# Expert layer of a four-layer kernel: router pieces, the low part and the spreads take other places in VectorE's and TensorE's step

## The reference, cut to what matters

```python
raw_scores = einsum('bsd,ed->bse', u, centroids)           # 16 experts
s = softmax(raw_scores + expert_biases)
topk_vals, topk_idx = top_k(s, 2)
g_topk = sum(one_hot(topk_idx, 16) * topk_vals[..., None], axis=-2)
xe = einsum('bsd,eod->bseo', u, Wr) + br
routed = einsum('bse,bseo->bso', g_topk, xe)
shared = (einsum('bsd,eod->bso', u, Ws) + sum(bs)) / 2
return u + routed + shared
```

## Time and profile before

| | |
|---|---|
| time, median of 3 runs | 1394.78 us (1393.96 to 1395.35) |
| the profiled execution: time, its span | 1394.4 us, 1392.2 us |
| TensorE matmuls busy | 1273.8 us (91% of the span) |
| VectorE, ScalarE, GpSimd busy | 996.3, 768.2, 519.3 us |
| expert layer, from its first spread to its last pair | 322.6 to 523.2 us of the span |

### The profile page before, as it was taken

The page is one execution under the profiler, slowest core; times in us unless marked ns, Lnnn a source line. Parts: engine busy times, 40 slices in busy tenths (PEclk is TensorE's granted clock), DMA queues, the critical chain, the costliest instruction groups (busy, mean ns, idle before and its releaser), DMA issues.

```text
span 1392.2 us, 31560 instructions
## 1 busy us (share of the span) xinstructions
PE 1273.8 (91%) x10330; PEld 1050.0 (75%) x10330; DVE 996.3 (72%) x2481; ACT 768.2 (55%) x2324; POOL 519.3 (37%) x687
## 2 busy tenths in 40 slices
PE   3999999987898896999999999999999977899997
PEld 2777777767888885777777777777777755899997
DVE  5466666656888886767777777777777764788886
ACT  2233333322222222988888888888888886444442
POOL 3243333334454455434445454444444431111111
PEclk9999999997999998999999999999999999999999
DMA  8000000000000000000000000000000000000000
GB/s 266 1 1 1 0 0 0 0 1 1 1 0 0 0 1 1 2 1 2 1 2 2 0 0 0 0 0 0 0 0 0 1 1 1 1 12 11 11 11 17
DMA packets 14445, 12.30 MB, mean 9 GB/s; under 512 B 1922, under 2 KB 12708, under 8 KB 14116
## 3 DMA queue, kind: packets, MB, share of 16 engines
q1 hardware_dynamic: 14372, 11.35, 2.6%
HBM read 9.25 MB, written 2.10 MB: 8 GB/s over the span
## 4 chain that ended last, share of the span: by engine, by line
PE 55%; DVE 18%; issue 11%; ACT 9%; POOL 4%; DVEq 1%; POOLq 0%; ACTq 0%
PE bank L935 9%; PE bank L171 8%; PE bank L528 8%; PE bank L477 6%; PE bank L1015 6%; ACT work L952 6%; PE bank L1028 5%; PE bank L800 4%; DVE work L944 3%; PE bank L986 3%; DVE stat L278 2%; ACT work L972 2%; POOL rstd L345 2%; PE bank L755 2%; DVE work L1180 1%
## 5 line engine op out<-in xcount | busy, mean ns | idle before, releaser
L952 ACT ACTIVATE work<-bank,work 128x256 f32<-128x256 f32 x512 | 234.8, 485 | 70.4 <-DVE work L944 70.4
L944 DVE TENSOR_REDUCE work<-bank 128x2 f32<-128x512 f32 x256 | 158.8, 682 | 131.6 <-PE bank L935 131.6
L918 POOL TENSOR_TENSOR work<-work 128x512 f32<-128x512 f32 x128 | 160.6, 1276 | 88.9 <-DVE work L908 88.9
L343 POOL TENSOR_SCALAR ve<-mv 128x2 f32<-128x2 f32 x128 | 28.6, 223 | 362.5 <-DVE mv L283 362.5
L972 ACT ACTIVATE work<-work 128x256 f32<-128x256 f32 x384 | 161.5, 535 | 0.0
L966 POOL TENSOR_TENSOR work<-work 128x512 f32<-128x512 f32 x64 | 66.6, 1040 | 251.1 <-DVE work L960 251.1
L935 PE MATMUL bank<-work 32*128 32x256 f32 x2048 | 130.5, 391 | 14.3 <-ACT XnT L372 9.6
L486 DVE TENSOR_TENSOR la_work<-bank,tri 128x512 f32<-128x512 f32 x128 | 87.6, 684 | 77.3 <-PE bank L477 77.2
L986 PE MATMUL bank<-ident,work 128*128 128x128 f32 x1024 | 137.7, 277 | 2.3 <-ACT work L994 1.3
L1015 PE MATMUL bank<-work 128*64 128x256 f32 x1024 | 126.5, 388 | 14.0 <-DVE work L1001 14.0
L800 PE MATMUL bank<-WrT,moe_work 128*128 128x128 f32 x1024 | 137.6, 278 | 0.7 <-POOL moe_work L777 0.7
(11 more groups left out here) (170 smaller groups left out, 2924.2 us busy)
## 6 DMA issues: line engine op xcount, KB each, us to landing
X<-in_x SPq DMA_DIRECT2D x4, 512.0 KB, 6.1
wF<-in_L_ffn_h_w SPq DMA_DIRECT2D x2, 1024.0 KB, 9.8
out<-X SPq DMA_DIRECT2D x16, 128.0 KB, 1.8
w_qkv<-in_L_attn_w_qkv SPq DMA_DIRECT2D x1, 1536.0 KB, 8.9
WrT<-in_L_ffn_Wr SPq DMA_DIRECT2D x1, 1024.0 KB, 4.9
w_out<-in_L_attn_w_out SPq DMA_DIRECT2D x1, 512.0 KB, 10.2
wF<-in_L_ffn_w_w SPq DMA_DIRECT2D x2, 256.0 KB, 8.6
rope_sin<-in_rope_sin SPq DMA_DIRECT2D x1, 256.0 KB, 2.8
```

The costliest lines, as they stand in the source:

```text
L918: nc.gpsimd.tensor_tensor((QT if kind == "q" else KT)[:, p, a, :], rc[:, ru % 2, :], rs_[:, ru % 2, :], ALU.add).then_inc(c_rope, 1)
L944: nc.vector.tensor_reduce(nmax[:, QUAD * a + j, :], SB_[j][:, :].rearrange("p (t k) -> p t k", t=T), AX.X, ALU.max, negate=True).then_inc( ...
L952: ins = nc.scalar.activation(pr[:, a % 2, j, t, :], SB_[j][:, t * LEN:(t + 1) * LEN], ACT.Exp, bias=nmax[:, h, t:t + 1], accum_out=psum_[: ...
```

## The change

On VectorE the late router parts move from behind pair 4 to before it, right behind norm 1. Pair 5 moves behind norm 2, low from behind norm 4 to right behind pair 5. Early 0 comes before norm 5, early 1 right behind it, next 0 after that; early 2 comes before next 1 in place of after it, and early 3 and next 2 change places. On TensorE the transposes of the gates come after pair 1 and its spread in place of pair 2, and the next sequence's first four spreads go behind pairs 5, 6, 6 and 7 in place of 4, 5, 6 and 7. The work is the same, instruction for instruction.

```diff
-        MOE_ORDER = (("norm", 0), ("norm", 1), ("pair", 4), ("late", 4), ("late", 5), ("late", 6), ("late", 7), ("pair", 5),
-                     ("norm", 2), ("pair", 6), ("norm", 3), ("norm", 4), ("low", 0), ("norm", 5), ("next", 0),
-                     ("early", 0), ("norm", 6), ("norm", 7), ("early", 1), ("next", 1), ("early", 2), ("norm", 8),
-                     ("early", 3), ("next", 2))
+        MOE_ORDER = (("norm", 0), ("norm", 1), ("late", 4), ("late", 5), ("late", 6), ("late", 7), ("pair", 4), ("norm", 2),
+                     ("pair", 5), ("low", 0), ("pair", 6), ("norm", 3), ("norm", 4), ("early", 0), ("norm", 5), ("early", 1),
+                     ("next", 0), ("norm", 6), ("norm", 7), ("early", 2), ("next", 1), ("norm", 8), ("next", 2),
+                     ("early", 3))
...
                     elif more:
-                        moe_spread_tensor(pe, i + 1, 1 - p, k - 4)
+                        for k2 in ((), (0,), (1, 2), (3,))[k - 4]:
+                            moe_spread_tensor(pe, i + 1, 1 - p, k2)
                     if k == 0 and not i_is(i, 0, 1):
                         norm_tensor(pe, 2, i - 2)
-                    if k == 2 and more:
+                    if k == 1 and more:
                         moe_gates_tensor(pe, i + 1, 1 - p)
```

## The result

The changed kernel takes 1402.55 us (median of 6 runs, 1400.71 to 1404.75) against 1395.07 for the kernel before in the same comparison: a ratio of 1.0053, 95% interval 1.0040 to 1.0066. It is slower, as forecast, by 7.5 us, and 2.3 us above the forecast time of 1400.3 (the forecast's sum had +5.8). The profiled execution of the changed kernel took 1400.71 us, its span is 1398.8 us against 1392.2.

The account below looks back on a forecast made before the run. The prediction took a ring of VectorE and GpSimd as the bound. Twelve loop steps at +0.43 (+5.2 us) and +0.6 outside the loop made +5.8 on 1394.4, stated as 1400.3 us, with an 80% range of 1393.2 to 1402.8.

Parts of the forecast that it names:

- a ring with TensorE in slack: Expert layer loop: VectorE and GpSimd set the 12.59 us step; filling TensorE's 1.27 us hole gives nothing unless the ring shortens.
- Closing the holes: VectorE's step: the 0.48 hole before norm 3 goes, the one before norm 5 exceeds 1 us, about 0.3 appears before norm 8.
- TensorE's margin for VectorE's pair 6: Gates' transposes hold pair 2, spread 6 and VectorE's pair 6 at 3.87; ready by 3.8 at worst, the tightest margin, 0.1 us.
- The step's +0.43: End of VectorE's step: early 3's CAST is held until GpSimd's L777 ends, lengthening each loop step by 0.43 us; chance 0.56.
- the rival in which only L703 is held: At early 3 the product L703 is held but the CAST is not: +0.25 a step, +3.4 in all, 1397.9; chance 0.10.
- The sum: Whole kernel: twelve loop steps +5.2 us and four steps outside the loop +0.6, together +5.8; forecast time 1400.3 us.
- The four steps outside the loop: Steps 0, 1, 14 and 15 have only part of the loss: between -0.05 and +0.45 each, together +0.6 us.
- The next layer has nothing to absorb it: Behind the expert layer: the next layer starts from the last norm 8, so nothing of the +5.8 us is absorbed.
- That nothing is held: No hold at early 3, as L777 comes after it or the two don't exclude each other: 1393.7, no change; chance 0.17.
- That the late parts are held as well, or the gates' margin is gone: Late parts beside GpSimd, or gates' transposes on TensorE: 12 x 0.2 us more, 1403; chance 0.04.
- L323 might come first at norm 5: L323 ahead of L777: norm 5 about 0.6 instead of 1.40, 12 x -0.4, 1389.6; chance 0.08.
- TensorE as the bound: TensorE bounds the kernel after all and its 15.2 us wait goes: 1379; chance 0.05.

Follow-up runs that it names:

- the half product: Changed kernel with GpSimd's product L777 of pair 3 covering one expert of two in sequences 1 to 15 (128x256 instead of 128x512): 1395.16 us, ratio 1.0003.
- early 3 moved: Changed kernel with early 3 (L700, L703) right behind early 2 instead of at the end of VectorE's step: 1392.19 us, ratio 0.9979 to the kernel before.
- TensorE's part: Kernel before with only the change's TensorE order (gates behind pair 1, first spreads behind pairs 5, 6, 6, 7): 1398.32 us, ratio 1.0027.
- VectorE's part: Kernel before with only the change's VectorE order, TensorE's order as before: 1401.24 us, ratio 1.0044.
- both holds out: Changed kernel with early 3 behind early 2 and GpSimd's product of pair 7 waiting for norm 5: 1377.54 us, ratio 0.9871 to the kernel before.

## Why the prediction was right, point by point

**The bound.** VectorE and GpSimd were read as a ring with TensorE in slack. Right: TensorE's 15.2 us wait was removed and the step grew; and the ring's own arithmetic gave the new places of norm 2 to norm 8 to within 0.3 us. Norm 3 and norm 5 are the 0.3 late in step 6: norm 2 is 0.08 late, and low was taken at 0.35 because starts overlap ends, but no such overlap stands around it (pair 5 at 405.48, low at 406.19, pair 6 at 406.64: 1.16 us where 0.96 was summed).

**Closing the holes.** The 0.48 before norm 3 went, the one before norm 5 grew to 0.98 and 0.92 (above 1 forecast), a new one of 0.17 stood before norm 8 (0.3 forecast). Right, with the sizes somewhat off. TensorE's margin for VectorE's pair 6, which I put at 0.1 us, held: no wait stands there.

**Early 3.** The step's +0.43 was measured as +0.44 (26.06 less 25.18, halved), but its parts differ. The CAST is held, from 0.17 to 0.65 and 0.74 in the two steps of an iteration; of the bounds it was the upper one, and the rival in which only L703 is held is out. L777 comes 1.90 and 2.00 us behind early 2 where I had 1.89 from the earlier trace rows. The next piece follows the CAST's end by 0.18 inside an iteration and by 0.52 at its turn, where 0.28 was taken for both. The extra time of an iteration (0.22, of which 0.18 before pair 4) was said to stay in its first step; it did in size but now lies at the turn, as 0.26 before L278: the two steps are 12.95 and 13.11, not 13.1 and 12.9.

The prediction reads from its rows that small VectorE instructions are held until GpSimd's instruction ends. None of the meetings in them is one of a CAST, so for early 3 this was the author's estimate. Beside L777 the runs show it, the run with the half product most directly (the product is 0.64 us long, and the CAST ends 0.03 behind it). Beside GpSimd's power L345 they do not: products of two SBUF tiles ran beside it in 0.16 and 0.23 us, as without it (rows in the last section). What sets the two GpSimd instructions apart is not shown.

**The sum.** The sum itself is not closed: 1394.4 plus 5.8 plus the 0.4 by which the median was said to lie above the profiled execution is 1400.6, not 1400.3. Twelve loop steps: +5.2 forecast, +4.65 measured, since the first of them did not grow (12.97 before, 12.96 after) and the last, behind which the loop does not turn, grew by 0.30 (12.49 to 12.79). The four steps outside the loop: +0.6 forecast, +0.3 measured. "The next layer has nothing to absorb it" is the step that was mis-sized: the layer behind did not absorb, it added. From the last norm 8 to the first scores it is 1.1 us more and to the end 1.7. In the profiled executions the 4.9 of the expert layer and these 2.8, less 1.1 in the layer before, make +6.6; the medians differ by 7.5, and single executions can't settle the 0.9 between the two. So the expert layer paid 0.9 less than the 5.8 forecast for it, and the stretches behind it, put at nothing, paid 2.8. That the total came out only 1.7 above the forecast sum is in part luck, and at 1402.55 the time lies just inside the upper end of the range, 1402.8.

That opening takes 22.4 to 22.5 us in the changed kernel and in the runs with early 3 moved, the half product, TensorE's part and VectorE's part, and 21.2 to 21.4 in the kernel before and the other four. Nothing in it was changed. The granted clock of TensorE differs there between the kernel before and the changed one. Both in 5 us stretches, the kernel before first (the third column from the end is the granted clock, as a share):

```profile
525.00:530.00 5.00, 4.67 (x21) 4.05 (x21) 2.26 (x8) 1.16 (x2) 2.65 (x4) 0.70 0.00 0
...
550.00:555.00 5.00, 3.73 (x20) 2.40 (x20) 3.78 (x9) 4.69 (x19) 1.10 (x2) 0.91 0.01 2
```

```profile
530.00:535.00 5.00, 5.00 (x28) 4.58 (x28) 2.38 (x7) 1.20 (x2) 1.76 (x2) 0.73 0.00 0
...
550.00:555.00 5.00, 4.29 (x33) 3.36 (x34) 0.93 (x3) 0.00 (x0) 1.72 (x2) 0.50 0.01 3
555.00:560.00 5.00, 4.79 (x20) 3.90 (x19) 3.84 (x9) 4.79 (x19) 1.21 (x2) 0.50 0.01 2
```

In both TensorE stands idle at the end of the expert layer, 1.93 us before the last transposes, and behind that the granted clock goes from 1.00 to 0.50: in the kernel before at 527.0 us, 1.9 behind the start of these transposes (525.09), in the changed kernel at 529.3, 0.4 behind it (528.90). In the kernel before the first projections still run at 1.00 (the second of the rows below in 0.39 us) and the fall comes behind them, in the changed kernel the first ones run at 0.50 (the second in 0.63 us):

```profile
525.77 0.47 PE L171 MATMUL bank<-w_hi,sx_lo 128*128 128x512 f32 x1 [0.24 <-POOL sx_lo L861]
526.08 0.39 PE L171 MATMUL bank<-w_lo,sx_hi 128*128 128x512 f32 x1
```

```profile
529.58 0.77 PE L171 MATMUL bank<-w_hi,sx_lo 128*128 128x512 f32 x1 [0.23 <-POOL sx_lo L861]
530.14 0.63 PE L171 MATMUL bank<-w_lo,sx_hi 128*128 128x512 f32 x1
```

VectorE's first rotation waits for these, 3.67 us in place of 2.64. From the first of these matmuls to that rotation it is 1.91 us before and 2.93 after, which is 1.0 of the 1.1 us. The other runs fall in line: that first matmul takes 0.76 or 0.77 us in all five executions with the long opening and 0.47 in all five with the short one. So the 1.1 us goes with the moment at which the clock falls. What sets that moment is open, and with one profiled execution of each kernel it is not known either whether it belongs to the kernel or to the execution: neither TensorE's order (the run with both holds out has the new one and 21.2 us) nor VectorE's alone decides it. The 1.7 us behind it is not explained either; over all ten profiled executions that stretch varies from 845.6 to 848.3 us in no clear relation to the edits. Part of it may be the clock, which is back at 0.91 at 550 to 555 us before and still at 0.50 at 555 to 560 us after, 5 us further on; that was not tested.

**The rivals.** That only L703 is held: out. That nothing is held: out by the runs that change the hold. That the late parts are held as well, or the gates' margin is gone: out, L710, L714 and L721 take 0.16, 0.23 and 0.23 in the changed kernel, as alone. That L323 might come first at norm 5 for itself: it did not, L777 still wins by 0.07 us; when it was made to, the step gained 0.66 (12.59 to 11.93) and 0.77 (12.27 to 11.50), near the 0.8 of that rival. TensorE as the bound: out.

## What to carry to other kernels

Before moving a small VectorE instruction, look at what GpSimd does at the new place: a cast of 128x4 elements behind a 1.09 us GpSimd product is a 0.74 us instruction. In a ring of engines a wait that is removed elsewhere brings nothing (TensorE's 15.2 us here), and "busy" grows with no more work (0.85 us an iteration here), so follow the ring and not the longest wait in the list. And where two engines hold each other, let the one go first that the ring passes through: here one added wait on GpSimd gave 10.7 us.

## What the runs showed of the hardware that was not expected

The hold also works the other way round: in the run with early 3 moved, L777 started while VectorE's L323 ran (0.33 behind its start) and took 1.21 us in place of 1.09. In the other step of the iteration it started 0.44 behind L323 and took 1.10.

```profile
399.40 1.21 POOL L777 TENSOR_TENSOR moe_work<-moe_work,XnT 128x512 f32<-128x512 f32 x1 [0.66 <-ACT moe_work L771]
```

GpSimd's power L345 (0.71 us, its operands in SBUF) held nothing: the products L710 and L714 ran beside it in 0.16 and 0.23 us in the kernel before.

```profile
416.35 0.71 POOL L345 TENSOR_TENSOR rstd<-ve,nhalf 128x2 f32<-128x2 f32 x1
416.53 0.16 DVE L710 TENSOR_TENSOR moe_work<-moe_work 128x4 f32<-128x4 f32 x1
416.73 0.23 DVE L714 TENSOR_TENSOR moe_work<-moe_work 128x64 f32<-128x64 f32 x1
```

And VectorE stands idle for 0.26 us at the turn of a loop whose body ends in an instruction of 0.23 us. In the kernel before, whose body ends in one of 0.69, nothing is visible there; 0.15 us stands idle one piece later, before pair 4 (0.22 us more in that step than in the other). Why is not shown.
